# Products of a zero tile in the idle time of TensorE, in the heads and waits inside the stages of a four-layer decoder

## What is computed

```
att = einsum('bhqd,bhkd->bhqk', q, k) * scale + bias      # L0_attn (causal), L2_attn (band)
att = softmax(att); y = einsum('bhqk,bhkd->bhqd', att, v)
sim = einsum('bhqd,bhfd->bhqf', q*scale, k)               # L0_xattn: 8 heads of 64, keys = context and latents
...                                                       # L1_xattn: the softmax goes over the heads
...                                                       # L2_xattn: two additive biases per head, two masks
...                                                       # L3_xattn: 16 heads of 16, no mask
out = experts of the routed tokens                        # L1_ffn (three relu layers), L2_ffn (gated, and a shared one)
h = bit_linear(quantised x, ternary w1); conv; bit_linear(h, ternary w2)   # L3_ffn
```

## Time and profile before

| | us |
|---|---|
| three runs | 2248.95, 2252.06, 2265.27 |
| median | 2252.06 |
| the profiled execution, its own time | 2243.71 |
| its span | 2241.8 |
| TensorE busy in it | 1845.6 |
| VectorE busy | 1481.2 |
| ScalarE busy | 1078.9 |
| GpSimd busy | 795.1 |

### The profile page before, as it was taken

The page is one execution under the profiler, slowest core; times in us unless marked ns, Lnnn a source line. Parts: engine busy times, 40 slices in busy tenths (PEclk is TensorE's granted clock), DMA queues, the critical chain, the costliest instruction groups (busy, mean ns, idle before and its releaser), DMA issues. The chain is left out here.

```text
span 2241.8 us, 32360 instructions
## 1 busy us (share of the span) xinstructions
PE 1845.6 (82%) x11379; PEld 909.1 (41%) x11379; DVE 1481.2 (66%) x2572; ACT 1078.9 (48%) x1949; POOL 795.1 (35%) x680
## 2 busy tenths in 40 slices
PE   5888979999776777777897788999788786899954
PEld 3445423333544444445584552333156534122223
DVE  4544256664565999995435548999654455788676
ACT  3454124545333555552344343888833434266746
POOL 1000025555144999993305012666641312000011
PEclk8899989999887999997897899999979897699967
DMA  6611552210009115003415734331045400444000
GB/s 199 150 40 66 194 185 66 66 34 15 20 26 249 42 24 95 2 1 115 158 58 173 190 83 97 81 72 41 15 157 184 157 10 17 105 111 96 13 1 19
DMA packets 174404, 192.10 MB, mean 86 GB/s; under 512 B 15844, under 2 KB 140335, under 8 KB 173335
## 3 DMA queue, kind: packets, MB, share of 16 engines
q1 hardware_dynamic: 171172, 181.64, 29.5%
q0 software_dynamic: 3072, 8.39, 1.2%
HBM read 125.61 MB, written 68.30 MB: 86 GB/s over the span
## 5 line engine op out<-in xcount | busy, mean ns | idle before, releaser
L3468 POOL TENSOR_TENSOR a2x_masked<-a2x_masked,tall_rows 128x512 f32<-128x512 f32 x128 | 163.2, 1276 | 126.1 <-ACT a2x_masked L3430 126.1
L1561 ACT ACTIVATE experts<-a1x_scores 128x512 f32<-128x512 f32 x256 | 132.2, 602 | 138.2 <-PE a1x_scores L1483 138.2
L3479 DVE TENSOR_REDUCE a3x_row_most<-a3x_ring 128x1 f32<-128x512 f32 x256 | 162.9, 684 | 26.0 <-PE a3x_ring L3318 24.9
L3479 DVE TENSOR_REDUCE a2x_row_most<-a2x_ring 128x1 f32<-128x512 f32 x256 | 162.1, 679 | 4.9 <-PE a2x_ring L3321 4.9
L1598 POOL TENSOR_TENSOR a1x_tree<-experts 128x1024 f32<-128x1024 f32 x64 | 150.6, 2352 | 37.2 <-ACT experts L1561 34.8
L854 DVE TENSOR_REDUCE ctx_then_heads<-a0x_rows 128x2 f32<-128x1024 f32 x88 | 107.7, 1223 | 82.0 <-PE a0x_rows L689 81.8
L671 POOL TENSOR_TENSOR a0x_pair_sums<-a0x_probs_T 128x1024 f32<-128x1024 f32 x48 | 114.7, 2389 | 129.6 <-ACT a0x_probs_T L800 102.2
L1531 DVE TENSOR_REDUCE a1x_most<-a1x_scores 128x128 bf16<-128x2048 f32 x64 | 145.8, 2278 | 14.9 <-PE a1x_scores L1474 14.9
L1522 DVE TENSOR_TENSOR experts<-experts,a1x_inverse_total 128x2048 f32<-128x2048 f32 x64 | 145.5, 2274 | 1.0 <-ACT a1x_inverse_total L1573 1.0
L3423 ACT ACTIVATE a3x_probs_T<-a3x_scores_T 128x1024 f32<-128x1024 f32 x128 | 123.1, 1018 | 46.7 <-PE a3x_scores_T L3345 46.6
L3423 ACT ACTIVATE wide_rows<-a2x_masked 128x1024 f32<-128x1024 f32 x128 | 135.9, 1061 | 1.4 <-POOL a2x_masked L3468 1.4
(11 more groups left out here) (674 smaller groups left out, 4220.3 us busy)
## 6 DMA issues: line engine op xcount, KB each, us to landing
v_scr<-p0x_vout SPq DMA_DIRECT2D x24, 256.0 KB, 2.0
k_scr<-p0x_x SPq DMA_DIRECT2D x24, 256.0 KB, 2.3
ctx_then_heads<-k_scr SPq DMA_DIRECT2D x8, 768.0 KB
a0x_vs<-v_scr SPq DMA_DIRECT2D x8, 768.0 KB, 4.7
experts<-in_L_ffn_w SPq DMA_DIRECT2D x8, 768.0 KB, 6.6
v_scr<-experts SPq DMA_DIRECT2D x16, 256.0 KB, 2.2
a1x_vs<-v_scr SPq DMA_DIRECT2D x16, 256.0 KB, 4.6
v_scr<-m1f_vout SPq DMA_DIRECT2D x16, 256.0 KB, 2.5
```

The costliest lines, as they stand in the source:

```text
L1561: nc.scalar.activation(ex[:, n % E, 4 * i:4 * i + 4, :], sp_[:, bank(n, i), :, :], ACT.Exp).then_inc(expd, 1)
L3468: nc.gpsimd.tensor_tensor(sm[:, i % 2, 1, :], sm[:, i % 2, 1, :], full[1][:, i // 2 % KT, :], ALU.add).then_inc(pool_masked, 1)
L3479: nc.vector.tensor_reduce(rm[:, u % 2, h * QT + qt:h * QT + qt + 1, part], ring[:, row_place(r) % 3, 0:n], AX.X, ALU.max).then_inc(row_mos ...
```

## The change

A bf16 tile `zeros` of 128 x 512 is added, and filled with zeros by GpSimd in the first stage. A helper issues n matmuls of the bf16 identity with it into a bank, with no wait and no semaphore. It is called at these places:

```
+def keep_going(core, bank, n):
+    for _ in range(n):
+        core.nc.tensor.matmul(bank, core.ident_bf[:, :], core.zeros[:, :], start=True, stop=True, skip_group_check=True)
...
 norm_stage, after the raw transposes
+                if raw_T is not None:
+                    keep_going(core, tp[:, 0, :], 9)
...
 wide_attention_stage
+                keep_going(core, up[:, :], 8)
                 pe.wait_ge(minus_in, 1)
                 done = 0
                 for i in range(NR):
                     row(i)
+                    keep_going(core, up[:, :], 2)
+                keep_going(core, up[:, :], 10)
...
 head_softmax_stage, before the first score
+                keep_going(core, up[:, :, :], 20)
...
 routed_relu_stage, after the key products
+                keep_going(core, odd_y[:, :], 40)
...
 routed_glu_stage, after `counted`, and after the key products
+                keep_going(core, odd_h[:, :], 18)
...
+                keep_going(core, odd_h[:, :], 22)
...
 bit_in_stage, a bank of its own, after the last product
+        spare = st.ps("spare", [P, 512])
...
+                keep_going(core, spare[:, :], 45)
...
 quad_attention_stage
                 for r in range(NR):
                     row(r)
+                    keep_going(core, sT[:, 0, 0, :], 1)
                 turn_most(0)
+                if nkey == T:
+                    keep_going(core, sT[:, 0, 0, :], 14)
                 for r in range(NR, lead):
                     row(r)
+                    keep_going(core, sT[:, 0, 0, :], 1)
```

More of the change, by code:

```diff
@@ L93, in __init__ @@
         self.ones = sb("ones", [P, P])
+        self.zeros = sb("zeros", [P, 512], BF16)
         self.causal = sb("causal", [P, 2, P], BF16)
@@ L178, in _ @@
                 end_prefetch(sp, loads, loaded)
+            if tiles_in:
+                @block.gpsimd
+                def _(pool):
+                    nc.gpsimd.memset(core.zeros[:, :], 0.0)
             @block.vector
```

1 line of the change is left out of this document (added).

## The result

The change makes the kernel slower: 2266.0 us in the median of 17 runs, against 2252.5 for the kernel before in as many. The ratio is 1.0066, with a 95% interval of 1.0048 to 1.0084, so +15 us (+11 to +19). It lies within 1% of no change, as most of the chance said, but outside the range, and on the other side of the forecast (-2.4).

What follows compares the result with a forecast made beforehand. No engine was taken to bound the whole; VectorE or TensorE paces the attention stages by turns. Gaps -6.4 and heads +4.0 sum to -2.4 us, 2252.1 to 2249.7 us, range 2238 to 2262.

Steps and rivals of the forecast that it cites:

- The step that failed: Head of a3x: products raise the clock early, VectorE then paces and the first scores run warm; -3.5 us.
- rival 3: Head of a3x alone stays cold because its row is thin: +10.5 there, 2264 us in all; chance 0.06.
- The rule of the Trainium skill: Head of a3x: only idle gaps above about 3 us matter, so products mend nothing; the sum becomes +2.6.
- The other heads: Heads of a0a, a2a and a2x: a product behind each row delays the first scores by +2.4, +2.6 and +2.5 us.
- The gaps: Waits in media, a0x, a1x, m1f, m2f and b1: products fill them and warm the work behind; -6.4 us together.
- a1x: Gap in a1x: 20 products start the first scores 2.0 us late, warmth gives back 1.5; +0.5, between -1.5 and +4.
- m2f: Gaps in m2f: gain of the first 18 products hidden, the 22 behind the key products warm the experts; -0.6 us.
- That zeros count: All places: products with zero operands count as work for whatever sets the clock, judged from the head of a2x.
- rival 2: All places: products of zeros don't raise the clock; about +96 us, 2348 us in all; chance 0.07.

Runs made afterwards that it cites:

- e5: Kernel before, plus one product of the row's own thin shape (16 partitions) per row in the head of a3x; ratio 1.0013, median 2253.6 us against 2251.3.
- e10: Kernel before, with rows and steps of a3x over all 96 partitions and one product of zeros per row in its head; ratio 1.0022.
- e6: Kernel before, plus two full products of zeros beside each row in the head of a3x; ratio 1.0175, median 2290.5 us against 2251.3.
- e7: Kernel before, plus the 44 products in the head of a3x alone, with ones instead of zeros; ratio 1.0094, median 2272.6 us against 2251.3.
- e8: Kernel before, plus 20 products ahead of the first row of a3x and none beside the rows; ratio 1.0039, median 2262.7 us against 2251.3.
- e2: Kernel before, plus the 44 products in the head of a3x alone; ratio 1.0122, median 2275.3 us against 2254.4.
- e1: The change without the 44 products in the head of a3x; ratio to the kernel before 1.0010, median 2255.5 us against 2254.4.
- e9: Kernel before, with rows and steps of a3x over all 96 partitions instead of 16, no products; ratio 1.0026.
- e3: Kernel before, plus only the 196 products in the gaps (media, a0x, a1x, m1f, m2f, b1); ratio 0.9957, median 2243.1 us against 2254.4.
- e12: Kernel before, plus 176 gap products in media, a0x, m1f, m2f and b1, none in a1x; ratio 0.9958, median 2243.2 us against 2250.0.
- e4: Kernel before, plus only the 132 products in the heads of a0a, a2a and a2x; ratio 1.0016.

## Why the prediction was wrong

**The step that failed** is the one on a3x, "With a product the row is 0.85 cold and TensorE has no idle time, like the start of a2x, so I expect the level to rise". Both halves were wrong. The row was 1.07, because a product over 128 partitions next to a matmul over 16 costs 0.535 and not 0.43 (e5: 0.40 from row to thin product; e10: 0.43 with both full). And the clock did not rise, not with one product, nor with two (e6), nor with ones (e7), nor did it last when it was high before (e8); it rose with full rows and a product (e10). The term was put at -3.5; in the trace it is +20.8 in the head and +3.0 behind it, and the three traces with these products (after, e2, e7) agree on it to 0.1 us. In the runs it is +13 (the change less e1), +21 (e7, with ones) or +27 (e2). Why the clock did not rise stays open: the thin rows and the time lost at the changes of shape were there together.

**The rival that came true** is the third, the head of a3x alone staying cold, which had 0.06. It was priced with the wrong row: 44 x 0.85 = 37.6 against 27.1, +10.5. The right one is 44 x (1.07 - 0.60) = 20.7. The rows of before spoke for it: 27.1 us of the head at 0.50 with TensorE marked as busy for 24.97 of them is a place where being busy had not raised the clock. I read this as the fault of pauses. The busy time itself does not tell a thin matmul from a full one; and the pauses do count, as e9 shows, but to close them with full products between thin rows was not enough.

**The rule of the Trainium skill** on idle gaps ("TensorE: Matmul & The Clock Gate", section "Why this matters for your kernels"), weighed in the prediction, gave for this place that products have nothing to mend. Its sum, +2.6, has the right sign and is nearer to the measured +15, but far from it. The rule is about a clock that is up, and the head of before began cold, so that row was no test of it. The trace of e8 is one, and there it isn't enough: the clock was at 1.00, no pause was longer than 0.57 us, and it fell. A long gap fits the rule: behind 5.9 us of idle time e8's first products were cold (0.70 over the twenty).

**The other heads** were right in kind and a little small. Forecast +2.4, +2.6 and +2.5 to the first scores; the traces have +3.7, +3.3 and +3.6. In a2x a row was the 0.65 forecast, and 3 of them were cold in 3.8 us. What the forecast left out is the turn of the maxima behind the 32nd row: TensorE, now the engine that paces, stops 0.8 us for VectorE's last reduction, and 1.1 us pass between the product ahead of the turn and the next row. In a0a and a2a the 14 products went behind a turn that was already 3 to 4 us late, and little or nothing was left of the wait that they were to fill (3.2 and 4.5 us). (The prediction's own sum for a2a, 3.0 + 3.0 against 4.5, is 1.5 and not 1.3, and its total 2.8.) Over whole stages a2a and a2x keep their loss, and in a0a it can't be seen: the table below has all fourteen traces.

**The gaps** were right in sign and somewhat small: -6.4 forecast, -10 (-4 to -16) in e3, -9 (-4 to -15) in e12. Fourteen traces lie at hand, and each stage has products in some of them and none in the others, so what the products are worth can be read without leaning on one execution. From the first real matmul of the stage to that of the next (for b1 with b2 to the last matmul), in us, the median and the range:

| stage | without products | with | difference | forecast |
|---|---|---|---|---|
| media | 16.4 (16.2 to 16.6) | 15.2 (15.2 to 15.4) | -1.2 | -1.0 |
| a0x | 272.3 (272.1 to 272.9) | 270.3 (270.2 to 270.3) | -2.0 | -1.7 |
| m1f | 159.3 (155.4 to 159.8) | 157.6 (157.3 to 158.4) | -1.7 | -2.0 |
| m2f | 139.7 (133.8 to 140.0) | 136.8 (136.5 to 137.4) | -2.9 | -0.6 |
| b1, b2 | 83.3 (83.0 to 84.4) | 82.0 (81.6 to 82.3) | -1.3 | -1.6 |
| a0a | 116.5 (112.9 to 120.1) | 116.6 (115.9 to 120.6) | +0.1 | +2.4 |
| a2a | 87.7 (84.5 to 90.2) | 90.2 (90.0 to 90.5) | +2.5 | +2.6 |
| a2x | 273.2 (272.9 to 274.6) | 276.6 (276.5 to 277.7) | +3.4 | +2.5 |

The first five add up to -9.1, which fits the -10 and -9 of the runs. a1x, the sixth place, comes out at about nothing: its first score is 1.3 us later behind the stage before than in the trace of before (forecast 2.0), and it takes 1.3 less from there (forecast 1.5). The term that was too small is m2f. Its 18 products made `m2f_op` 2.0 us shorter, which I had put down as hidden by GpSimd's scatters. The experts' first turns started 1.1 earlier for it and their steady loop 1.9: so the tokens' load, too, had waited for something behind TensorE. What, no run takes apart.

**That zeros count** was right (e8, and m1f for holding), and rival 2, which ended slowest, did not happen. The time did stay within 1% (0.88), but its sign was the other. The range should have reached to rival 3 at its true price: the forecast of 2250, the 3.5 of a3x not gained and 20.7 lost, 2274. Added up from the traces, the change should cost 21 us (-9.1 in the gaps, +6.0 in the three heads' stages, +23.8 in a3x), which is above the +15 (+11 to +19) of the runs. That rest stays unexplained.

## What to carry to other kernels

Filling a wait of TensorE with products of zeros is worth what the work behind it loses at the low clock, and it is safe where the wait is longer than the products at the clock that holds when they are issued; here that was -10 us of 2250 from 196 products. Between real matmuls it is another matter: count the row with its product at both clocks against the engine that paces, and add the change of shape. And before counting on the clock to rise, look for a stretch of the same kernel with the same kind of matmul where it did rise; where a stretch with busy TensorE stayed low for its whole length, find out first what it is that does not count.

## What the runs showed of the hardware

At 1.2 GHz a matmul of 512 columns over 128 partitions next to one over 16 is 0.53 to 0.54 us from start to start (after, e2, e6). Among full ones it is 0.43 (e10), among thin ones in the same half 0.40 (e5). At 2.4 GHz the same is seen in a0x of the kernel after, whose rows contract over 64 partitions and run two side by side:

```profile
302.46 0.39 PE L703 MATMUL a0x_rows<-ctx_then_heads 64*128 64x512 bf16 x2
302.78 0.60 PE L141 MATMUL a0x_u<-zeros,ident_bf 128*128 128x512 bf16 x2
303.32 0.39 PE L703 MATMUL a0x_scores_T<-ctx_then_heads 64*128 64x512 bf16 x2
303.64 0.60 PE L141 MATMUL a0x_u<-zeros,ident_bf 128*128 128x512 bf16 x2
```

In the kernel before, a pair of such rows with no product behind it takes 0.22 us:

```profile
314.56 0.38 PE L689 MATMUL a0x_rows<-ctx_then_heads 64*128 64x512 bf16 x2
314.78 1.02 PE L711 MATMUL a0x_scores_T<-ctx_then_heads 64*128 64x512 f32 x4
```

With the products it is 0.32, and the two products behind it are 0.54 for 2 x 0.22. So each change costs about 0.1 us, as much time as at 1.2 GHz. It is hidden there, since VectorE paces.

In a3x the granted clock was 0.50 through 66 us in which TensorE waited for nobody (e6). A TensorE that never waits is therefore not enough for the high level. Where it rose early in a head (a2x in the traces of before and after, a3x in e10), matmuls over 96 to 128 partitions followed each other directly, 0.43 us apart.

The steps of one and the same stage came up to 1.00 after 10 to 14 us in four executions and after 38 in another (e4), which alone is 10 us. What decides it is open.
